# Cutting two VectorE operations per block into four, in the segment reduction of a graph network on one core

## The reference

```python
# gcn (layers 0 and 3): rows of a table summed over the edges of a node
out = jax.ops.segment_sum(h[src] * norm[:, None], dst, num_segments=n)
# edge convolution (layer 2, four times): the maximum over the edges of a node
agg = jax.ops.segment_max(msg, dst, num_segments=n)      # msg: rows of x[src], x[dst] through weights
# layer 1: edge features through a small network, times h[src], summed over dst
agg = jax.ops.segment_sum(h[idx_j] * Wij, idx_i, num_segments=n)
```

## Time and profile before

| what | value |
|---|---|
| median of 3 runs | 10620.65 us |
| the profiled execution's own time | 10631.74 us |
| its span (first to last instruction) | 10630.0 us |
| POOL busy, share of the span | 8032.4 us, 76% |
| DVE busy, share of the span | 4419.4 us, 42% |
| DMA engines busy, mean | about 33% in most slices |

### The profile page before, as it was taken

The page is one execution under the profiler, slowest core; times in us unless marked ns, Lnnn a source line. Parts: engine busy times, 40 slices in busy tenths (PEclk is TensorE's granted clock), DMA queues, the critical chain, the costliest instruction groups (busy, mean ns, idle before and its releaser), DMA issues. The chain is left out here.

```text
span 10630.0 us, 49732 instructions
## 1 busy us (share of the span) xinstructions
PE 1639.5 (15%) x9025; PEld 1437.8 (14%) x9025; DVE 4419.4 (42%) x9272; ACT 543.8 (5%) x1417; POOL 8032.4 (76%) x7137
## 2 busy tenths in 40 slices
PE   2000048888860000100001000100001000010000
PEld 1000047777750000100001000100001000010000
DVE  4444434444443444344443444334444444444444
ACT  2000021111130000000000000000001000000000
POOL 4777768888847777677776777777777777777777
PEclk7555567777775555555555555555555555555555
DMA  5444435555532333333333333323333333333333
GB/s 190 142 142 142 145 88 77 77 74 76 77 86 91 95 95 95 99 95 95 95 97 97 95 95 95 101 93 95 95 95 98 96 95 95 95 100 95 95 95 104
DMA packets 467313, 1064.01 MB, mean 100 GB/s; under 512 B 156534, under 2 KB 276192, under 8 KB 412586
## 3 DMA queue, kind: packets, MB, share of 16 engines
q0 software_dynamic: 320736, 464.07, 19.8%
q1 hardware_dynamic: 143480, 597.45, 15.5%
q10 hardware_dynamic: 2940, 1.00, 0.0%
HBM read 517.80 MB, written 552.72 MB: 101 GB/s over the span
## 5 line engine op out<-in xcount | busy, mean ns | idle before, releaser
L991 POOL DMA_INDIRECT WORK<-table,S x5824 | 6249.0, 1073 | 2037.5 <-issue 1772.7
L1045 DVE TENSOR_TENSOR Z<-WORK,RESET 128x512 f32<-128x512 f32 x612 | 423.5, 692 | 2615.7 <-DMA WORK<-table,S 2601.8
L1210 POOL DMA_INDIRECT acc<-TOT,stage x832 | 1300.8, 1564 | 276.0 <-issue 207.6
L1090 PE MATMUL bank<-ident,WORK 128*128 128x128 f32 x7 | 3.3, 474 | 8069.6 <-DVE WORK L1074 8069.6
L1045 DVE TENSOR_TENSOR Z<-WORK,KEEP 128x512 f32<-128x512 f32 x459 | 317.6, 692 | 1958.9 <-DMA WORK<-table,S 1948.5
L1090 PEld LDWEIGHTS bank<-ident,WORK 128*128 128x128 f32 x7 | 1.3, 183 | 8071.1 <-DVE WORK L1074 8071.1
L1048 DVE TENSOR_TENSOR WORK<-WORK,Z 128x512 f32<-128x512 f32 x1071 | 741.0, 692 | 36.5
L1064 DVE TENSOR_TENSOR WORK<-WORK,Z 128x1536 f32<-128x1536 f32 (+2 forms) x448 | 633.8, 1431 | 12.4
L1059 DVE TENSOR_TENSOR Z<-WORK,S 128x1536 f32<-128x1536 f32 (+2 forms) x448 | 633.6, 1431 | 12.3
L1415 DVE SCALAR_TENSOR_TENSOR BASE<-bank,WEIGHT,BASE 128x128 f32<-128x128 f32 x832 | 234.2, 344 | 839.8 <-PE bank L1285 772.3
L1053 DVE SCALAR_TENSOR_TENSOR WORK<-WORK,S 128x128 f32<-128x128 f32 x1428 | 502.5, 352 | 50.9
(11 more groups left out here) (247 smaller groups left out, 2663.4 us busy)
## 6 DMA issues: line engine op xcount, KB each, us to landing
run_rows<-WORK SPq DMA_DIRECT2D x357, 1024.0 KB, 4.1
WORK<-table,S POOLq DMA_INDIRECT x5824
fill_rows<-BASE SPq DMA_DIRECT2D x52, 1024.0 KB, 6.8
WORK<-fill_rows SPq DMA_DIRECT2D x104, 512.0 KB
table<-TF SPq DMA_DIRECT2D x56, 384.0 KB
WORK<-carry_rows SPq DMA_DIRECT2D x49, 384.0 KB
acc<-TOT,stage POOLq DMA_INDIRECT x832
acc<-Z SPq DMA_DIRECT2D x12, 1024.0 KB
```

Of the source, the lines that this page charges most:

```text
L991: pool.indirect_dma_start(RING_T[:, b * WIDE + k, :], None, table, table_row(table, INDEX[:, t:t + 1]))\
L1045: step(dve.tensor_tensor(TMP[:, 0:groups, 0, :], rows[:, :, j - 1, :], mask(keep[:, :, j], groups, 0), op0))
L1210: pool.indirect_dma_start(acc_dram[a], bass.IndirectOffsetOnAxis(stage[:, h, j % HALF:j % HALF + 1].bitcast(u32), 0), TOT[:, j // QUAD % 2 ...
```

## The change

`spans` is cut differently. A regular block has two operations of 768 numbers where it had one of 1536, in L1059 and again in L1064. A ring-start block has 384, 768 and 384 where it had 384 and 1152. So every block has four operations in place of two, or six in place of four. `steps` counts them. Nothing else is changed.

```diff
-            steps = 6 + GROUPS + 2
+            steps = 6 + GROUPS + 4
...
                     wait(dve, reduced, n)
-                    spans = [(0, groups)] if first else [(0, 1), (1, groups)]
+                    spans = [(0, 2), (2, groups)] if first else [(0, 1), (1, groups - 1), (groups - 1, groups)]
                     for a, b in spans:
                         ends = RING_T[:, (first + FOUR * a - 1) % SPAN:, :][:, 0:FOUR * (b - a - 1) + 1:FOUR, :]
                         step(dve.tensor_tensor(TMP[:, a:b, :, :],
```

## The result

The changed kernel takes 10654.11 us (median of 13 executions, 10647.15 to 10708.68) against 10623.39 for the kernel before: a ratio of 1.0036, 95% interval 1.0024 to 1.0048. It is 0.36% slower.

The account below looks back on a forecast made before the run. A pass was taken to last as long as POOL needs for 832 gathers, some held up by DVE operations. Gains of 194 us (regular blocks) and 27 (ring-start) made 221: 10620.65 - 221 = 10400 us, range 10380 to 10470.

Parts of the forecast that it names:

- The contact at 0.13 us after a gather's start: In each POOL gather (L991): about 0.13 us after starting, it waits for the running DVE operation.
- the release at the end of a DVE operation: A held gather goes on when the running DVE operation ends; the next contact follows 1.25 us later.
- the walk through the block: Stalls under L1059 and L1064: regular block 1.39 to 0.66 us, gain 194; ring-start 1.53 to 1.23, gain 27.
- The unknown: Whether a gather gets through between two DVE operations overlapping by 0.08 us; always (-221 us) was taken, chance 0.80.
- Durations of 768: A DVE operation of 768 numbers in L1059 or L1064 was put at 957 ns.
- the pitch: Two DVE operations of one line overlap by 0.08 us, so a pair of 768 takes 1.84 us.
- DVE's extra 57 us: The cuts make DVE work 0.08 us longer per line, 57 us in all, costed at nothing.
- the idle time of DVE covers them: DVE stands idle 12.7 us ahead of each block, so its longer work was expected to cost nothing.
- what is late next is POOL's own 0.944 + 0.30 per gather: With the stalls gone, only POOL's gather time and issue gap limit a pass, so all 221 us count.
- the pair that holds the gather like one operation: Rival at L1059 and L1064: no opening between the halves, +58 us, 10679 us, chance 0.10.
- The prediction's own test: L991's mean falls 38 ns to about 1035; if it falls and the time does not, POOL doesn't set a pass.

Follow-up runs that it names:

- e1: The changed kernel once more, nothing altered, for a second trace: 10656.56 us, ratio 1.0023 to the kernel before.
- e3: Changed kernel plus a POOL memset ahead of each block's thirteenth gather, bringing back the old pace: 10631.77 us, ratio 1.0001 to the kernel before.
- e12: Changed kernel plus a 0.62 us POOL pause in every block, without DVE's covered waits and spare semaphores: 10583.51 us, ratio 0.9963 to the kernel before.
- e6: Changed kernel, treatment varied by pass: L1059 cut alone, L1064 cut alone, or both cuts with POOL pauses in some blocks: 10653.21 us, ratio 1.0021.
- e7: Changed kernel with POOL pauses of 0.65 to 0.21 us in passes 1 to 5, three DVE waits dropped in pass 6; passes took 1131.7 to 1160.7 us.
- e13: Kernel before plus one-column ACT copies after each block, up to 64, number varied by pass: 11055.85 us against 10600.83.
- e11: Kernel before plus 0 to 16 one-column DVE operations with semaphores per block, by pass; passes 5 and 6 took 1158.7 and 1159.8 us.
- e5: Changed kernel, treatment varied by pass: half rows, stores or partitions, no L1059 and L1064, eight added DVE operations; 10700.48 us with work left out.

## Why the prediction was wrong

**What held.** The contact at 0.13 us after a gather's start, the release at the end of a DVE operation, and the walk through the block: 0.99 and 1.55 where 0.98 and 1.57 were forecast. The unknown, whether a gather gets through between two operations that overlap by 0.08 us, was taken as always, and so it came out: in the traces of the changed kernel, e1, e3 and e12 a gather got in at the end of the first of two overlapping operations more than 1800 times, and 2 of them (in e1) waited longer. In passes with a full record the stalls are down by 30 to 31 us a pass (from 107 to 77 in e3 and 76 in e12), 7 x 31 = 217 of 221 us. Durations of 768 (953 against 957 ns), the pitch (1.82 to 1.83 against 1.84) and DVE's extra 57 us (56) were right, and the idle time of DVE covers them, as e12 shows. The Trainium skill's page "SBUF — State Buffer" (section "SBUF: two separate sides") would by its "whole instruction" have left no opening, as the prediction read it; the 0.99 speaks against it.

**What failed** is the sentence behind the sum: all of it lies on the path, "what is late next is POOL's own 0.944 + 0.30 per gather". Something else was late next. The kernel before ran at 1146 / 832 = 1.377 us per gather; the changed one wanted 1.341. Between the two, at some 1.363 (21.8 us a block), the record of events turns thin, and then POOL is held at 1.400. So the term for what is late next was too small, and no row of the kernel before was given for it beyond the gather's own time. The saving was spent twice. In the pass itself 9 us of 31 remain, since the first 26 blocks are still fast and use up the slack. Behind the pass the semaphore of PE's first group of matmuls comes 32 us late, where it came 8 us late: the group has 24 matmuls, and 24 x 1.400 = 34 us, which fits one instruction in 1.400 us, though no run here changed their number. The five stages between passes cost 108 us more in e1; gained are 50 us in six passes, 31 in pass 0, 6 in the stage of the edges and 2 ahead of pass 0; 1 is lost behind the last pass. That leaves some 20 us lost, and e1's span is 10650.0 where it was 10630.0. By the medians of e1 and of the kernel before beside it 27 us are lost: 22 in the span (10650.05 against 10628.0) and 5 outside it (6.75 against 1.8).

**The profiled execution** of the changed kernel is 52 us longer because there pass 0 had a thin record as well: 22 us more in the pass, 30 behind it (1895.0 against 1864.7 us). Why pass 0 alone can stay full at 21.45 us a block is not known; it differs by the extra stores of its blank rows.

**The range.** It stopped at 10470, and the slower side had one rival in it, the pair that holds the gather like one operation, at 10679. The time lies near that, by another mechanism: no gather took the 1.8 to 1.9 us under L1059 that the rival needs. The prediction's own test came half true: the mean fell, to 1059 and not to 1035, and the time did not fall with it, so POOL's own 0.944 + 0.30 was not all that set a pass. One row of the kernel before could have been a warning: PE's semaphore reached ACT and DVE 8 us after its work was done, a wait put down to "remote" that the prediction did not read.

**Shown and argued.** Shown: two states, told apart by the events in the trace; the thin one comes on by pace (e3, e6, e7) and by added instructions of ACT at an unchanged pace (e13) or of DVE (e11); in it gathers, a pause, ACT's copies and DVE's small operations come at about 1.400 us. Argued: that the cause is the way that the reports take. The Trainium skill's page "NOTIFIC — the notification-queue block" (section 7.1) says of the unit that writes these records that its internal pipeline always holds the producers back rather than lose a record, which fits the engines' 1.400 us but not by itself the thin record, in which some 260 of 290 semaphore events a block are missing; its section 10 says that an emitted record costs the engine zero cycles, and by that no copy of ACT would have waited, where they took 1.40 in place of 0.09 us apiece. Every execution timed here, the medians included, has its spans and clocks recorded and shows the same times as the profiled ones (e1: 10650.77 to 10660.61, profiled 10656.05), so what the two cuts are worth where nothing is recorded was not measured. Open too: why the thin state tips at 21.8 us by pace and only beyond 379 counted reports a block at 22.07 (17.2 a microsecond, against 16.8 where e7's pass 4 turned), so that the reports don't weigh the same; why the steps are multiples of 0.70; and why in the last blocks of e6's passes 3 and 4 a pause no longer cost its 1.400.

## What to carry to other kernels

A stall that is taken away is a gain only up to the next limit, and that limit need not be an engine: when a faster stretch slows down again after a while, and to a round number of time per instruction, vary what could be counted (bytes, rows, instructions) one per stretch, and let an engine that does nothing run at it too. Waits that the profile can't name ("remote", "issue") on short stages are worth a look before a sum is booked in full, and so is a kernel's distance from the state in which its own records come thin. Where such a limit is near, part of the gain can be kept by pacing, but with a margin: 0.49 us of pause lost 0.35%, 0.62 us (with DVE's spare events left out) won 0.37%.

## What the hardware showed that was not expected

In the thin state an engine that had nothing to do with the gathers, ACT, got a copy through in 1.40 us where it takes 0.09, and the same 1.400 us stood between gathers and for a pause. The state is nearly all or nothing: in 104 of the 105 passes traced, blocks 20 to 23 have either 220 or more events a block on average or 35 or fewer; the one between is pass 6 of e5, which went to and fro. A gather gets in between two DVE operations that overlap by 0.08 us, in all but 2 of more than 1800 cases; and two cuts that together gain 31 us in a pass that keeps its record gain -5 and +1.5 us apart (1150.7 and 1144.5 against 1146).
